# The bilinear products of a graph layer in 32-row pieces: four column groups of TensorE in place of two

## The chip, the cores and the metric

The kernel runs on one NeuronCore of one Trainium2 chip. The metric is the device time of one execution in microseconds (us), median of 3 runs. One profiled execution gives the trace from which all rows are read.

## The reference

The input is x, 128 graphs of 64 nodes with 384 features, and adj, 128 matrices of 64 x 64 edge weights. Four residual blocks follow one another, each `x = x + block(relu(layernorm(x)), adj)`. Block L0 is an attention with 12 heads and adj as bias, L2 a directed graph layer done twice, L3 an attention with adj as mask. The change touches block L1 alone, a graph layer done twice (l = 0, 1):

```
m_left = h @ W_left[l].T;  m_right = h @ W_right[l].T
u_left = h @ m_left.T / sqrt(384);  u_right = h @ m_right.T / sqrt(384)      # 64 x 64 for each graph
u = u_left * triu(adj, 0) + u_right * transpose(triu(adj, 1))
delta = exp(u) * adj;  attention = delta / (sum(delta, 2) + 1e-10)
h = relu(layer_norm(attention @ (h @ W_lin[l].T + b_lin[l])) * a + b)
```

So of u_left only the entries on and above the diagonal count, and of u_right only those below it: of the 128 numbers that the two forms give for a node, the masks keep 64.

## The kernel before, in words

One program for one core runs the four blocks as phases, one after the other. Each phase takes the 8192 rows (128 graphs of 64 nodes) in 16 groups of 512 rows: 4 tiles of 128 rows, two graphs to a tile. Products with weights (`split_matmul`, L52) are made of three fp32r matmuls each, with operands split in a high and a low part. Products of activations with one another run in plain fp32.

The second phase is `bilinear_phase` (block L1). Its unit of work is one layer of one group, 32 units in all, numbered `number(i, k)`; k = 0 to 3 are group 0 and 1 of a turn in the first layer, then both in the second. The opening unit stands by itself, then a loop runs units k = 1, 2, 3, 4 seven times, and the last three units close. Each engine has its own hand-written order, and semaphores tie them. A unit is, on TensorE (`unit` in `@block.tensor`):

- six products `product(i, k, j)`, 9 matmuls of 512 columns each: m_left and m_right, transposed, into the PSUM tiles `psW[0]`, `psW[1]`; ScalarE copies each into the SBUF tile `m` (`m_part`, L1252);
- behind the last three of them a set of four 128 x 128 transposes each (`passed`, L1495) of the next unit's rows into `psT`; ScalarE writes them out twice (`hT_part`, L1245 or L1248) and VectorE makes the low part `hT_lo` (L1349);
- `linear(0)`, 9 matmuls of 384 columns, read out by VectorE (`lin_copy`, L1363);
- `bilinear(i, k, t)` for the four tiles t (L1530): for each tile, each of the 3 chunks c of 128 features and each graph g of the tile one fp32 matmul, whose stationary operand is the 64 nodes of h (`hT_whole`) and whose moving operand is the left and the right m of the same 64 nodes, 128 columns. The result goes to partitions 64g to 64g + 63 of `psU`;
- `linear(1)`, `linear(2)`, `linear(3)`;
- `context` (L1554), delta times the linear rows, 8 fp32 matmuls.

VectorE multiplies `psU` by the masks (`mask_u`, L1357), adds the halves (L1359), ScalarE takes the exponential (L1256), VectorE multiplies by adj (`weigh_adj`, L1368), and only then may `context` run. VectorE's order in a unit is: the statistics of the unit before, `passed(0)`, `passed(1)`, `passed(2)` (each a subtraction for `hT_lo`), `lin_copy(0)`, `mask_u`, `lin_copy(1)`, `weigh_adj`, `lin_copy(2)`, `lin_copy(3)`. GpSimd makes the masks ahead of time (`make_masks`, L1176) and does the roots and the affine part of the second layer's output.

The lines that the change works on:

```
m = sb("m", [P, 2, KC, COLS])
for c in range(KC):
    for g in range(2):
        nodes = slice(t * P + g * NODES, t * P + (g + 1) * NODES)
        ins = nc.tensor.matmul(psU[NODES * g:NODES * (g + 1), t * P:(t + 1) * P].rearrange("p (s n) -> p s n", s=2),
                               hT_whole[k % 2][:, c, nodes], m[:, :, c, nodes], ...)
```

In the trace an fp32 matmul of the program is two MATMUL records and two LDWEIGHTS records: the 24 matmuls of a unit's bilinear form are 48 records of each. A transpose is one record.

Of the kernel before, what the change touches and what calls it, by code (L numbers as in the profile page):

```python
# [21 lines left out]
ACT = mybir.ActivationFunctionType  # L22
AX = mybir.AxisListType

P = 128
GRAPHS, NODES, D = 128, 64, 384
KC = D // P
ROWS = GRAPHS * NODES
TILES = 4
COLS = TILES * P  # L30
# [946 lines left out]
def bilinear_phase(nc, ctx, shared, x_in, adj, adjT, x_out, a, next_weights):  # L977
# [2 lines left out]
    n_w = 6  # L980
    eps, var_scale = 1e-3, float(D) / (D - 1)
    PAIR = TILES // 2

    def sb(n, shape, dt=F32):
        return ctx.enter_context(nc.sbuf_tensor(f"l1_{n}", shape, dt))
# [4 lines left out]
    def sem(n):  # L990
        return ctx.enter_context(nc.semaphore(f"l1_{n}"))
# [2 lines left out]
    xr = [sb(f"xr{g}", [P, TILES, D]) for g in range(2)]  # L994
    hT = [(sb(f"hT{b}_hi", [P, KC, COLS], F32R), sb(f"hT{b}_lo", [P, KC, COLS], F32R)) for b in range(2)]
    hT_whole = [sb(f"hT_whole{b}", [P, KC, COLS]) for b in range(2)]
    m = sb("m", [P, 2, KC, COLS])

    rows_of = [sb(f"adj{k}", [P, TILES, NODES]) for k in range(4)]
    cols_of = [sb(f"adjT{k}", [P, TILES, NODES]) for k in range(4)]  # L1000
# [41 lines left out]
    m_done = sem("m_done")  # L1042
    m_set = sem("m_set")
    masks_set = sem("masks_set")
    u_done = sem("u_done")
    u_read = sem("u_read")
    u_set = sem("u_set")
# [24 lines left out]
    def is_first(i, k):  # L1072
        return isinstance(i, int) and i == 0 and k == 0
# [74 lines left out]
    @block.gpsimd  # L1148
    def _(pool):
        nc.gpsimd.memset(half[:, 0:1], -0.5).then_inc(zeroed, 1)  # L1150
        nc.gpsimd.memset(half[:, 1:2], 0.5).then_inc(zeroed, 1)
        nc.gpsimd.memset(lin[:, :, D:D + 1], 1.0).then_inc(zeroed, 1)
        nc.gpsimd.memset(tri[:], 1.0).then_inc(zeroed, 1)
        pool.wait_ge(zeroed, 4)

        def roots(i, g):
            pool.wait_ge(var_set, 2 * i + g + 1)
            nc.gpsimd.tensor_tensor(rstd[:, g, :], var[:, g, :], half[:, 0:1].broadcast_to([P, TILES]), ALU.pow)\
              .then_inc(rstd_set, 1)

        roots(0, 0)
        pool.wait_ge(rstd_set, 1)
        for s, (sign, compare) in enumerate(((-1, ALU.is_ge), (1, ALU.is_gt))):
            for g in range(2):
                part = tri[NODES * g:NODES * (g + 1), s, :]
                nc.gpsimd.affine_select(out=part, in_=part, compare_op=compare, fill=0.0, base=0,
                                        pattern=[[sign, NODES]], channel_multiplier=-sign).then_inc(zeroed, 1)
                pool.wait_ge(zeroed, 4 + 2 * s + g + 1)
        roots(0, 1)

        def make_masks(i, k):

            per_turn = 64 if k < 2 else 128
            pool.wait_ge(adj_in[k], i * per_turn + per_turn)
            for side, source in enumerate((cols_of[k], rows_of[k])):
                nc.gpsimd.tensor_tensor(masks[k][:, :, side, :], source[:],  # L1176
                                        tri[:, side:side + 1, :].broadcast_to([P, TILES, NODES]), ALU.mult)\
                  .then_inc(masks_set, 1)

        def root(i, k, p):  # L1180
            pool.wait_ge(c_var_set, 2 * number(i, k) + p + 1)
            pair = slice(PAIR * p, PAIR * (p + 1))
            nc.gpsimd.tensor_tensor(c_root[:, pair], c_mv[:, pair, 1], half[:, 1:2].broadcast_to([P, PAIR]), ALU.pow)\  # L1183
              .then_inc(c_root_set, 1)

        def affine(i, k, x):
            pool.wait_ge(rows_set, number(i, k) * TILES + x + 1)
            nc.gpsimd.tensor_tensor(act_rows[:, x, :], act_rows[:, x, :], ln_a[:], ALU.mult).then_inc(affine_set, 1)
            pool.wait_ge(affine_set, 2 * ((2 * i + k - 2) * TILES + x) + 1)
            nc.gpsimd.tensor_tensor(act_rows[:, x, :], act_rows[:, x, :], ln_b[:], ALU.add).then_inc(affine_set, 1)  # L1190

        def ending(i, k):

            root(i, k, 0)
            root(i, k, 1)
            if k >= 2:
                for x in range(TILES):
                    affine(i, k, x)

        def unit(i, k, ahead):  # L1200
            ending(i, k - 1)
            if ahead and k in (1, 2):
                roots(i + 1, k - 1)
            if ahead:
                make_masks(i + 1, k - 1)

        pool.wait_ge(consts, 80)
        for k in range(4):
            make_masks(0, k)

        def turn(i, ahead):
            for k in (1, 2, 3, 4):
                if k < 4:
                    unit(i, k, ahead)
                elif ahead:
                    unit(i, k, ahead)
                else:
                    ending(i, 3)

        with pool.Fori(0, last) as i:  # L1220
            turn(i, True)
        turn(last, False)

    @block.scalar
    def _(act):
# [23 lines left out]

        def m_part(i, k, j):  # L1250
            act.wait_ge(m_done, number(i, k) * 2 * KC + j + 1)
            nc.scalar.activation(m[:, j // KC, j % KC, :], psW[j % 2][:], ACT.Copy).then_inc(m_set, 1)  # L1252

        def exponential(i, k):
            act.wait_ge(u_set, number(i, k) + 1)
# [61 lines left out]
    def _(dve):  # L1317
# [43 lines left out]
        def lin_copy(i, k, t):  # L1361
            dve.wait_ge(lin_done, number(i, k) * TILES + t + 1)
            nc.vector.tensor_tensor(lin[:, t, 0:D], psW[t % 2][:, 0:D], b_lin[:, k % 4 // 2, :], ALU.add)\  # L1363
              .then_inc(lin_set, 1)
# [28 lines left out]
        def result(i, k, x):  # L1393
            g = k - 2
            if x == 0:
                dve.wait_ge(xr_in[g], (i + 1) * 16)
            dve.wait_ge(affine_set, 2 * ((2 * i + g) * TILES + x + 1))
            nc.vector.scalar_tensor_tensor(xr[g][:, x, :], act_rows[:, x, :], 0.0, xr[g][:, x, :], ALU.max, ALU.add)\
              .then_inc(y_set, 1)
# [8 lines left out]
        def unit(i, k, ahead):  # L1408
            tail = not is_first(i, k)
            nexts = k < 3 or ahead  # L1410

            def passed(c):
                if nexts:
                    hT_part((number(i, k) + 1) * KC + c, (k + 1) % 2, c)

            if tail:
                ending(i, k - 1)
            if ahead and k in (1, 2):
                statistics((i + 1, k - 1))
                variances(k - 1)  # L1420
            passed(0)
            passed(1)
            if ahead and k in (1, 2):
                shifts((i + 1, k - 1))
            if tail and k >= 3:
                result(i, k - 1, 0)
                result(i, k - 1, 1)
            passed(2)
            lin_copy(i, k, 0)
            mask_u(i, k)  # L1430
            lin_copy(i, k, 1)
            weigh_adj(i, k)
            lin_copy(i, k, 2)
            lin_copy(i, k, 3)
            if tail and k >= 3:
                result(i, k - 1, 2)
                result(i, k - 1, 3)

        statistics((0, 0))
        variances(0)  # L1440
        weights((0,))
        shifts((0, 0))
        statistics((0, 1))
# [28 lines left out]
    def _(pe):  # L1472
# [48 lines left out]
        def bilinear(i, k, t):  # L1521
            n = number(i, k)
            if t == 0:
                wait_apart(m_set, (n + 1) * 2 * KC)
                if not is_first(i, k):
                    wait_apart(u_read, n)
            for c in range(KC):
                for g in range(2):
                    nodes = slice(t * P + g * NODES, t * P + (g + 1) * NODES)
                    ins = nc.tensor.matmul(psU[NODES * g:NODES * (g + 1), t * P:(t + 1) * P].rearrange("p (s n) -> p s n", s=2),  # L1530
                                           hT_whole[k % 2][:, c, nodes], m[:, :, c, nodes],
                                           start=(c == 0), stop=(c == KC - 1))
            if t == TILES - 1:
                ins.then_inc(u_done, 1)

# [23 lines left out]
        def unit(i, k, ahead):  # L1559
            nexts = k < 3 or ahead  # L1560
            if not is_first(i, k):
                pe.wait_ge(hT_set, (number(i, k) + 1) * KC)
            if is_first(i, k):
                pe.wait_ge(w_lo_set, LEFT + 1)
            for j in range(2 * KC):
                if is_first(i, k) and j == KC:
                    pe.wait_ge(w_lo_set, RIGHT + 1)
                product(i, k, j)
                if nexts and j >= KC:
                    passed(i, k, j - KC)  # L1570
            if is_first(i, k):
                pe.wait_ge(w_lo_set, LIN + 1)
            linear(i, k, 0)
            for t in range(TILES):
                bilinear(i, k, t)
            linear(i, k, 1)
            linear(i, k, 2)
            linear(i, k, 3)
            context(i, k, 0)
            context(i, k, 1)  # L1580
# [848 lines left out]
```

## Time and profile before

| | |
|---|---|
| median of 3 runs | 2840.08 us (2840.01 to 2840.34) |
| the profiled execution | 2840.32 us |
| its span in the trace | 2838.6 us |
| TensorE (PE) busy | 2708.2 us, 95% of the span |
| VectorE (DVE) busy | 1802.0 us, 63% |
| ScalarE (ACT) busy | 1256.7 us, 44% |
| GpSimd (POOL) busy | 1093.8 us, 39% |
| mean granted TensorE clock | 0.978 |
| HBM read, written | 131.61 MB, 50.33 MB |

The profiled execution took 0.24 us more than the median of the runs, and 1.7 us more than its span. Busy shares are averages over four phases. PE is matrix multiplication, PEld its weight loads, which run beside it. A row of a timeline has a start, the time from the first start to the last end of the instructions merged in it, and their count (x48); a single MATMUL record lasts longer than the time until the next may start, since records overlap.

### The profile page before, as it was taken

The page shows a single profiled execution, that of the slowest core. Times are in us where ns is not written, and L with a number is a line of the kernel's source. Part 1 is how long each engine was busy: PE and PEld are TensorE (multiplying, and loading weights), DVE is VectorE, ACT ScalarE, POOL GpSimd, SP SyncE. Part 2 cuts the span into 40 slices and gives each one's busy share as a digit, 9 for nine tenths or more (in the row PEclk, how much of TensorE's full clock was granted, in tenths as well). Part 3 has the DMA queues.
Part 4 walks back from the last instruction along what each step waited for, and adds up shares of the span by engine and source line. Part 5 has one row for each costly group of instructions (what it writes and reads, how often), then busy time and mean ns, then how long its engine had stood idle before and what let it go on. Part 6 is the DMA issues. An engine that isn't in the chain of part 4 may idle for free. (4 is left out here: it accounts for less than half of the span.)

```text
span 2838.6 us, 75948 instructions
## 1 busy us (share of the span) xinstructions
PE 2708.2 (95%) x29582; PEld 2345.1 (83%) x29582; DVE 1802.0 (63%) x4227; ACT 1256.7 (44%) x2212; POOL 1093.8 (39%) x1081
## 2 busy tenths in 40 slices
PE   6999999986999999999958999999999978999998
PEld 5888888875888888888847888888888867888887
DVE  5777777764445545544546787787777765666565
ACT  3444444434443444444433334343343325565564
POOL 2333333342323322332232444443444443545455
PEclk9999999998999999999988999999999988999999
DMA  4222222214112112211121111111111112222221
GB/s 139 71 70 66 65 62 62 67 51 150 35 56 78 41 45 76 78 33 55 48 80 43 51 50 50 49 60 39 55 55 48 49 52 72 79 91 80 84 89 59
DMA packets 186659, 183.15 MB, mean 65 GB/s; under 512 B 79568, under 2 KB 186064, under 8 KB 186576
## 3 DMA queue, kind: packets, MB, share of 16 engines
q1 hardware_dynamic: 186576, 181.99, 20.9%
q8 instruction: 59, 0.97, 0.1%
q14 instruction: 24, 0.20, 0.0%
HBM read 131.61 MB, written 50.33 MB: 64 GB/s over the span
## 5 line engine op out<-in xcount | busy, mean ns | idle before, releaser
L52 PE MATMUL l_psW<-w_hi,l_hT_hi 128*128 128x384 f32 x1920 | 681.7, 355 | 2.0 <-DVE l_vX L573 2.0
L52 PE MATMUL l_psW<-w_hi,l_hT_lo 128*128 128x384 f32 x1920 | 647.6, 337 | 0.0
L52 PE MATMUL l_psW<-w_lo,l_hT_hi 128*128 128x384 f32 x1920 | 645.2, 336 | 0.0
L52 PE MATMUL l_psW<-l_hT_hi,w_hi 128*128 128x512 f32 (+1 forms) x1242 | 495.7, 399 | 12.1 <-ACT l_m L1252 3.7
L52 PE MATMUL l_psW<-l_hT_hi,w_lo 128*128 128x512 f32 (+1 forms) x1242 | 469.8, 378 | 0.0
L52 PE MATMUL l_psW<-l_hT_lo,w_hi 128*128 128x512 f32 (+1 forms) x1242 | 469.1, 378 | 0.0
L52 PEld LDWEIGHTS l_psW<-w_hi,l_hT_hi 128*128 128x128 f32 x1920 | 362.0, 189 | 38.5 <-issue 24.6
L52 PEld LDWEIGHTS l_psW<-w_lo,l_hT_hi 128*128 128x128 f32 x1920 | 362.6, 189 | 0.7
L52 PEld LDWEIGHTS l_psW<-w_hi,l_hT_lo 128*128 128x128 f32 x1920 | 361.4, 188 | 0.0
L52 PEld LDWEIGHTS l_psW<-l_hT_hi,w_hi 128*128 128x128 f32 x1242 | 236.0, 190 | 69.6 <-issue 22.1
L52 PEld LDWEIGHTS l_psW<-l_hT_hi,w_lo 128*128 128x128 f32 x1242 | 235.5, 190 | 44.8
L52 PEld LDWEIGHTS l_psW<-l_hT_lo,w_hi 128*128 128x128 f32 x1242 | 236.8, 191 | 35.3
L284 POOL TENSOR_TENSOR l_s_d<-l_s_b,l_mx 128x768 f32<-128x768 f32 x128 | 188.9, 1476 | 195.4 <-DVE l_mx L561 182.4
L1252 ACT ACTIVATE l_m<-l_psW 128x512 f32<-128x512 f32 x192 | 114.7, 598 | 324.0 <-PE l_psW L52 324.0
L1349 DVE TENSOR_TENSOR l_hT_lo<-l_hT_whole,l_hT_hi 128x512 fp32r<-128x512 f32 x96 | 87.4, 910 | 251.6 <-ACT l_hT_whole L1245 128.0
L1183 POOL TENSOR_TENSOR l_c_root<-l_c_mv,l_half 128x2 f32<-128x2 f32 x64 | 44.7, 698 | 461.7 <-DVE l_c_mv L1380 461.7
L1824 POOL TENSOR_TENSOR l_right<-l_right,l_b_r 128x384 f32<-128x384 f32 x128 | 132.4, 1038 | 113.3 <-ACT l_right L1902 113.3
L1829 POOL TENSOR_TENSOR l_c_scale<-l_c_var,l_half 128x2 f32<-128x2 f32 x64 | 51.5, 804 | 319.2 <-DVE l_c_var L2052 319.2
L295 POOL TENSOR_TENSOR l_xr<-l_xr,l_y_rows 128x384 f32<-128x384 f32 x64 | 64.2, 1003 | 258.8 <-ACT l_y_rows L401 258.8
L387 ACT ACTIVATE l_eT<-l_psP 128x768 f32<-128x768 f32 x128 | 104.0, 813 | 129.8 <-PE l_psP L750 126.4
L761 PEld LDWEIGHTS l_psS<-l_vX,l_eT 64*64 64x64 f32 x6144 | 103.1, 136 | 41.0 <-issue 37.1
L573 DVE TENSOR_TENSOR l_vX<-l_psW,l_bv 64x192 f32<-64x192 f32 x256 | 90.8, 355 | 61.0 <-PE l_psW L52 58.1
(160 smaller groups left out, 5145.8 us busy)
## 6 DMA issues: line engine op xcount, KB each, us to landing
after_l<-l_xr SPq DMA_DIRECT2D x192, 192.0 KB, 1.9
l_xl<-after_l SPq DMA_DIRECT2D x47, 768.0 KB, 4.7
l_xr<-after_l SPq DMA_DIRECT2D x32, 768.0 KB, 4.5
l_xl<-in_x SPq DMA_DIRECT2D x16, 768.0 KB, 4.8
l_xr<-in_x SPq DMA_DIRECT2D x64, 192.0 KB, 2.4
l_xr<-after_l SPq DMA_DIRECT2D x64, 192.0 KB, 2.3
out_x<-l_xr SPq DMA_DIRECT2D x64, 192.0 KB, 1.9
l_adj<-in_adj SPq DMA_DIRECT2D x48, 128.0 KB, 2.4
```

The costliest lines, as they stand in the source:

```text
L52: last = nc.tensor.matmul(out, lhs[a](c), rhs[b](c), start=(m == 0), stop=(m == n - 1))
L284: nc.gpsimd.tensor_tensor(s_d[:], s_b[:, t], mx[:, t, :].rearrange("p (h n) -> p h n", n=1).broadcast_to([P, HEADS, NODES]), ALU.subtract) ...
L295: nc.gpsimd.tensor_tensor(xr[:, t, :], xr[:, t, :], y_rows[:, t % 2, :], ALU.add).then_inc(y_set, 1)
L387: nc.scalar.activation(eT[:, :, :].rearrange("p a n -> p (a n)"), P_all, ACT.Copy).then_inc(eT_set, 1)
L573: ins = nc.vector.tensor_tensor(vX[part, t, g, :, 0:HD], src[:, :, b, :], bias, ALU.add)
L761: ins = nc.tensor.matmul(psS[NODES * g:NODES * (g + 1), r, S_end + c * (HD + 1):S_end + (c + 1) * (HD + 1)], eT[keys_b, a, NODES * g:NODES ...
L1183: nc.gpsimd.tensor_tensor(c_root[:, pair], c_mv[:, pair, 1], half[:, 1:2].broadcast_to([P, PAIR]), ALU.pow)\
L1252: nc.scalar.activation(m[:, j // KC, j % KC, :], psW[j % 2][:], ACT.Copy).then_inc(m_set, 1)
L1349: nc.vector.tensor_tensor(hT[b][1][:, c, :], hT_whole[b][:, c, :], hT[b][0][:, c, :].bitcast(F32), ALU.subtract)\
L1824: nc.gpsimd.tensor_tensor(right[:, t, :], right[:, t, :], b_r[:, u.layer, :], ALU.add).then_inc(right_set, 1)
L1829: nc.gpsimd.tensor_tensor(c_scale[:, pair], c_var[:, pair], half[:].broadcast_to([P, PAIR]), ALU.pow)\
```

## The change

The bilinear form is cut in halves of the nodes. The stationary operand is 32 nodes instead of 64, so that each matmul writes 32 partitions of `psU`, and the four matmuls of a tile and chunk (two graphs, two halves) write partitions 0 to 31, 32 to 63, 64 to 95 and 96 to 127. The tile `m` is laid out anew, with the 64 right columns of a graph ahead of its 64 left ones. The first half of the nodes then needs columns 0 to 95 of these 128 (all of the right, the first half of the left), the second half columns 32 to 127. So each matmul has 96 moving columns in place of 128, and a unit has 48 matmuls in place of 24. The 32 columns for each row that are no longer written are zero times mask: `psU` is set to zero once, on VectorE, at the start of the phase, and TensorE waits for that before the first form. The masks swap their two sides in the same way.

The last set of transposes, `passed(KC - 1)`, moves from behind the last product to behind `linear(0)`, just ahead of the bilinear form. VectorE's `lin_copy(0)` moves ahead of its `passed(2)`.

```diff
+    HALF = NODES // 2
...
-    m = sb("m", [P, 2, KC, COLS])
+    m = sb("m", [P, KC, 2 * TILES, 2, NODES])
...
+    u_zeroed = sem("u_zeroed")
...
-                nc.gpsimd.tensor_tensor(masks[k][:, :, side, :], source[:],
+                nc.gpsimd.tensor_tensor(masks[k][:, :, 1 - side, :], source[:],
...
-            nc.scalar.activation(m[:, j // KC, j % KC, :], psW[j % 2][:], ACT.Copy).then_inc(m_set, 1)
+            nc.scalar.activation(m[:, j % KC, :, 1 - j // KC, :], psW[j % 2][:].rearrange("p (g n) -> p g n", n=NODES),
+                                 ACT.Copy).then_inc(m_set, 1)
...
+            lin_copy(i, k, 0)
             passed(2)
-            lin_copy(i, k, 0)
             mask_u(i, k)
...
+        nc.vector.memset(psU[:], 0.0).then_inc(u_zeroed, 1)
         weights((0,))
...
-                if not is_first(i, k):
+                if is_first(i, k):
+                    wait_apart(u_zeroed, 1)
+                else:
                     wait_apart(u_read, n)
             for c in range(KC):
                 for g in range(2):
-                    nodes = slice(t * P + g * NODES, t * P + (g + 1) * NODES)
-                    ins = nc.tensor.matmul(psU[NODES * g:NODES * (g + 1), t * P:(t + 1) * P].rearrange("p (s n) -> p s n", s=2),
-                                           hT_whole[k % 2][:, c, nodes], m[:, :, c, nodes],
-                                           start=(c == 0), stop=(c == KC - 1))
+                    both = m[:, c, 2 * t + g].rearrange("p s n -> p (s n)")
+                    for lower in range(2):
+                        first = g * NODES + lower * HALF
+                        cols = slice(lower * HALF, lower * HALF + NODES + HALF)
+                        ins = nc.tensor.matmul(psU[first:first + HALF, t * P + cols.start:t * P + cols.stop],
+                                               hT_whole[k % 2][:, c, t * P + first:t * P + first + HALF], both[:, cols],
+                                               start=(c == 0), stop=(c == KC - 1))
...
-                if nexts and j >= KC:
+                if nexts and KC <= j < 2 * KC - 1:
                     passed(i, k, j - KC)
...
             linear(i, k, 0)
+            if nexts:
+                passed(i, k, KC - 1)
             for t in range(TILES):
                 bilinear(i, k, t)
```

TensorE, a unit of the loop, from the end of the last product to the start of `linear(1)`. Before (a row is one matmul of the program, or xN alike; ISA is a wait that stands by itself):

```order
L52 MATMUL l_psW<-l_hT_hi,w_lo 128x512
L1493 ISA
L1495 MATMUL l_psT<-ident,l_act_rows 128x128 x4
L1539 ISA
L52 MATMUL l_psW<-w_hi,l_hT_hi 128x384
L52 MATMUL l_psW<-w_lo,l_hT_hi 128x384
...
L52 MATMUL l_psW<-w_hi,l_hT_lo 128x384
L1530 MATMUL l_psU<-l_m,l_hT_whole 64x128 x24
L52 MATMUL l_psW<-w_hi,l_hT_hi 128x384
```

With the change:

```order
L52 MATMUL l_psW<-l_hT_hi,w_lo 128x512
L1548 ISA
L52 MATMUL l_psW<-w_hi,l_hT_hi 128x384
L52 MATMUL l_psW<-w_lo,l_hT_hi 128x384
...
L52 MATMUL l_psW<-w_hi,l_hT_lo 128x384
L1497 ISA
L1499 MATMUL l_psT<-ident,l_act_rows 128x128 x4
L1539 MATMUL l_psU<-l_m,l_hT_whole 32x96 x48
L52 MATMUL l_psW<-w_hi,l_hT_hi 128x384
```

The 24 matmuls of 64 x 128 (output rows x columns) have become 48 of 32 x 96, and the four transposes have moved past `linear(0)` to stand directly ahead of them.

VectorE, the same stretch in the opening unit. Before:

```order
L1349 TENSOR_TENSOR l_hT_lo<-l_hT_whole,l_hT_hi 128x512 x3
L1363 TENSOR_TENSOR l_lin<-l_psW,l_b_lin 128x384
L1357 TENSOR_TENSOR l_u_parts<-l_psU,l_masks 128x512
L1359 TENSOR_TENSOR l_u_sum<-l_u_parts 128x256
L1363 TENSOR_TENSOR l_lin<-l_psW,l_b_lin 128x384
L1368 TENSOR_TENSOR l_delta<-l_e_u,l_adjT 128x256
```

With the change:

```order
L1352 TENSOR_TENSOR l_hT_lo<-l_hT_whole,l_hT_hi 128x512 x2
L1366 TENSOR_TENSOR l_lin<-l_psW,l_b_lin 128x384
L1352 TENSOR_TENSOR l_hT_lo<-l_hT_whole,l_hT_hi 128x512
L1360 TENSOR_TENSOR l_u_parts<-l_psU,l_masks 128x512
L1362 TENSOR_TENSOR l_u_sum<-l_u_parts 128x256
L1366 TENSOR_TENSOR l_lin<-l_psW,l_b_lin 128x384
```

The third subtraction for `hT_lo` now stands between the copy of `linear(0)` and the masking of `psU`.

## Rows read from the trace of the kernel before

**Rows 1.** The page, busy time of the engines over the span

```profile
PE 2708.2 (95%) x29582; PEld 2345.1 (83%) x29582; DVE 1802.0 (63%) x4227; ACT 1256.7 (44%) x2212; POOL 1093.8 (39%) x1081
```

**Rows 2.** Stretches, 684.00:1459.90 is the second phase from its first form

```profile
core 0: us, PE busy (x) PEld busy (x) DVE busy (x) ACT busy (x) POOL busy (x), PEclk, DMA share, GB/s
684.00:1459.90 775.90, 774.49 (x5225) 641.83 (x5225) 386.34 (x1025) 333.33 (x578) 234.70 (x252) 1.00 0.18 53
```

**Rows 3.** Waits of the PE in that stretch: the only one

```profile
PE l_psC L1554 <- issue: 0.2, 1, 0.2
```

**Rows 4.** Timeline of the PE, one unit, from the last product on

```profile
start us, us, engine line op out<-in xcount [idle before <-releaser]
1003.64 0.40 PE L52 MATMUL l_psW<-l_hT_hi,w_lo 128*128 128x512 f32 x1
1003.88 0.60 PE L1495 MATMUL l_psT<-ident,l_act_rows 128*128 128x128 f32 x4
1004.23 0.42 PE L52 MATMUL l_psW<-w_hi,l_hT_hi 128*128 128x384 f32 x1
1004.49 0.34 PE L52 MATMUL l_psW<-w_lo,l_hT_hi 128*128 128x384 f32 x1
...
1005.71 0.34 PE L52 MATMUL l_psW<-w_hi,l_hT_lo 128*128 128x384 f32 x1
1005.98 2.84 PE L1530 MATMUL l_psU<-l_m,l_hT_whole 128*64 128x128 f32 x48
1008.75 0.44 PE L52 MATMUL l_psW<-w_hi,l_hT_hi 128*128 128x384 f32 x1
1009.03 0.33 PE L52 MATMUL l_psW<-w_lo,l_hT_hi 128*128 128x384 f32 x1
...
1013.65 1.89 PE L1554 MATMUL l_psC<-l_lin,l_delta 64*64 64x385 f32 x16
```

**Rows 5.** The tile psU: durations in ns, minimum/median/maximum

```profile
L1530 PE MATMUL l_psU<-l_m,l_hT_whole x1536: 272/273/324, 683.9 to 1453.4; 128*64 128x128 f32 x192
L2199 PE MATMUL l_psU<-l_hT_whole x1536: 221/222/367, 1494.7 to 2302.0; 128*64 128x64 f32 x192
```

**Rows 6.** The line of the context, the same columns

```profile
L1554 PE MATMUL l_psC<-l_lin,l_delta x512: 482/494/536, 691.6 to 1459.9; 64*64 64x385 f32 x171
```

**Rows 7.** Timeline of the PE in the third phase, its u in 64 columns

```profile
1530.08 1.62 PE L2199 MATMUL l_psU<-l_hT_whole 128*64 128x64 f32 x48
```

**Rows 8.** Timeline of the PE in the first phase, scores and weighing

```profile
102.57 0.90 PE L761 MATMUL l_psS<-l_vX,l_eT 64*64 64x33 f32 x48
...
119.15 1.28 PE L743 MATMUL l_psS<-l_kT,l_qT 32*64 32x64 f32 x96
```

**Rows 9.** The line of the scores, durations in ns

```profile
L743 PE MATMUL l_psS<-l_kT,l_qT x6144: 210/218/365, 36.6 to 2820.7; 32*64 32x64 f32 x199
```

**Rows 10.** Timeline of the weight loads beside the form of that unit

```profile
1005.98 2.60 PEld L1530 LDWEIGHTS l_psU<-l_m,l_hT_whole 128*64 128x64 f32 x48 [0.25 <-issue]
```

**Rows 11.** Timeline of ACT in that unit

```profile
1004.07 0.60 ACT L1252 ACTIVATE l_m<-l_psW 128x512 f32<-128x512 f32 x1 [0.59 <-PE l_psW L52]
1004.57 0.77 ACT L1245 ACTIVATE l_hT_hi<-l_psT,l_ln_bT,l_ln_aT 128x512 fp32r<-128x512 f32 x1
1005.23 0.78 ACT L1245 ACTIVATE l_hT_whole<-l_psT,l_ln_bT,l_ln_aT 128x512 f32<-128x512 f32 x1
```

**Rows 12.** Timeline of DVE in that unit

```profile
1006.04 0.69 DVE L1349 TENSOR_TENSOR l_hT_lo<-l_hT_whole,l_hT_hi 128x512 fp32r<-128x512 f32 x1 [1.76 <-ACT l_hT_whole L1245]
...
1008.94 0.69 DVE L1357 TENSOR_TENSOR l_u_parts<-l_psU,l_masks 128x512 f32<-128x512 f32 x1 [1.74 <-PE l_psU L1530]
...
1011.11 0.41 DVE L1368 TENSOR_TENSOR l_delta<-l_e_u,l_adjT 128x256 f32<-128x256 f32 x1
```

**Rows 13.** Timeline of DVE at the start of the phase

```profile
648.41 1.35 DVE L1324 TENSOR_TENSOR w_lo<-w_raw,w_hi 128x1152 fp32r<-128x1152 f32 x1
650.67 0.16 DVE L1344 SCALAR_TENSOR_TENSOR l_nbias<-l_mv,l_rstd 128x4 f32<-128x4 f32 x1 [0.91 <-POOL l_rstd L1158]
```

## Prediction

> **What bounds the kernel now.** I read the page first, then the stretch of the phase that the change touches, then the waits in it, then one unit in order of time. The page has PE busy for 95% of the span, and no other engine above 63% [rows 1]. Averages over four phases prove little, so the stretch decides: from the first bilinear form of the second phase to its end PE is busy 774.49 of 775.90 us, at a granted clock of 1.00, that is 2.4 GHz, while DVE works 386, ACT 333 and POOL 235 us [rows 2]. In all of it PE waited once, 0.2 us [rows 3]. So the second phase is PE's own work laid end to end, and a microsecond taken from PE there comes off the span, as long as nothing else becomes late. The reader is to see in the unit's timeline that the bilinear form starts at 1005.98, and the next matmul stands at 1008.75: 2.8 us in each of 32 units, some 90 us of the phase [rows 4].
>
> **What a record of the form costs.** An fp32 record of 128 columns lasts 272 ns at the least, one of 64 columns 221, one of 385 columns 482 [rows 5, 6]. That is 0.80 to 0.82 ns for each further column, two cycles at 2.4 GHz, so 128 columns hold their part of the array for about 107 ns; the rest is latency that overlaps. 48 records one after another would take 48 x 107 ns = 5.1 us. The form takes 2.84 us from first start to last end, less 0.27 for the last record: 2.57 us from first start to last start [rows 4, 5]. So two records, those of graph 0 and graph 1 on partitions 0 to 63 and 64 to 127, run at a time: 24 rounds at some 107 to 109 ns. The third phase's form, the same 48 records of 128 rows and 64 output rows with 64 columns, takes 1.62 - 0.22 = 1.40 us, 24 rounds at 58 ns [rows 5, 7].
>
> **The change, part by part.**
>
> 1. *The form.* 96 records, each on a quarter of the array's output side, with 96 moving columns. If four run at a time as two do now, that is again 24 rounds, now of 96 columns. The trace has such rounds for 64 columns (1.40 us) and for 128 (2.57 us), and 96 is halfway: 1.98 us from first to last start, and the last record lasts 247 ns in place of 273. Saved are 2.57 - 1.98 = 0.59, plus 0.03, together 0.61 us in each unit; 32 units give **19.6 us**. Both ends of this term come from the same rows: four starts in a round in place of two cost a few ns more or less. If a round is 3 ns off, the 24 x 32 rounds give 2.3 us either way.
>
> 2. *Do four run at a time?* No row of 128 rows of stationary data shows more than two. What is nearest: the scores run eight pieces of 32 x 64, 96 records in 1.28 - 0.22 = 1.06 us, 11 ns to a record, and the weighing four pieces of 64 x 64, 48 records in 0.90 - 0.22 = 0.68 us, 14 ns to a record [rows 5, 8, 9]. So the array does run four and eight at a time, and starts come far closer than the 1.98 us / 96 = 21 ns that the new form wants. But in both of these at most two records read the same partitions at once, in the new form four do. I take four at a time, because pieces side by side are what every such row shows; what it is worth if it fails is below.
>
> 3. *The weight loads.* 96 loads of 32 columns in place of 48 of 64, the same columns in all. They lie beside the matmuls now: 48 loads fill 2.60 us inside the form's 2.84 [rows 4, 10]. In the 64-column form two loads of 64 columns fit in every 58 ns. A round of the new form has four loads of 32 columns, as many columns, and 83 ns. If loads go by columns, they are covered: zero. If they went by the piece, they would not be (a rival, below).
>
> 4. *The transposes, moved.* In their old place they cost their own work: from their start at 1003.88 to the second matmul behind them at 1004.49 is 0.61 us, four at 109 ns and one matmul at 0.17 [rows 4]. Into the form some 0.10 us is lost (0.27 from the last start of linear(0), less 0.17), and behind it 0.20 us (1008.55 last start, plus 0.11, to 1009.03 less 0.17). The change of the array's pieces happens as often as before. Behind transposes the way into the form could cost nothing, or twice as much: 31 units x 0.10 us, 3.1 us either way. I take zero, since all that changes is which full-array work stands ahead.
>
> 5. *What becomes late by that move.* The third pair of ACT writes started at 1004.57, 0.7 us behind the start of its transposes, and ended at 1006.01 [rows 4, 11]. The transposes now start nine matmuls later, 1.57 us, so ACT ends near 1007.6, and DVE's subtraction, 0.69 us, near 1008.3 [rows 12]. It now stands ahead of the masking. The form ends 0.61 us earlier, and masking, which started at 1008.94, could start at 1008.33 [rows 12]. Hence a delay of 0.0 to 0.1 us for DVE. Who waits for it: the exponential, then delta at 1011.11 to 1011.52, then the context on PE at 1013.65, 2.1 us later [rows 4, 12]. That cover holds also when both ends move 0.6 us forward. The first unit's `hT_lo` is wanted only by the next unit's products, 6 us later. Zero. Were the cover gone, each 0.1 us would cost 3 us.
>
> 6. *Copies, masks, zeroing.* ACT writes m in eight pieces of 64 columns; at 0.60 us against a product's 2.1 us and with ACT at 43% of the stretch, some 10% more would be hidden [rows 2, 11]. The masks only swap sides. The zeroing of `psU` is one DVE instruction on 512 columns, not longer than the 0.69 us that masking the same tile takes [rows 12]. It stands ahead of the split of the first weights, behind which DVE waits 0.91 us for POOL's root [rows 13]. Zero, at most a tenth.
>
> Sum: 2840.3 us of the profiled execution less 19.6 gives 2820.7; the median of the runs stands 0.2 lower, so **2820.5 us**. In this case alone the range is 2815 to 2826 (2.3 for the rounds, 3.1 for the transposes).
>
> **Rivals.**
>
> - *Four cannot run at a time on the same 128 partitions, two can.* Then 96 records of 96 columns are 48 rounds at 83 ns, 4.0 us, against 2.57: 1.4 us more in each unit, 46 us in all: **2886 us**. For it: two is the most that any row has on one partition. Against it: nothing in the trace shows a limit at two; it is only never tried. It decides the sign: with s records at a time the form takes 96 x 83 ns / s, which is 2.57 us at s = 3.1. So below three at a time the change loses. Chance 0.07.
> - *A record has a price of its own.* The densest starts of records with 128 rows are 1.40 us / 48 = 29 ns [rows 7]. If that is the price of a load or a start whatever its columns, 96 of them take 2.79 us, 0.2 us more than now, **2847 us**. Against it stand the 11 and 14 ns of the first phase [rows 8], with fewer rows. Chance 0.06. The Trainium skill, page "TensorE: Matmul & The Clock Gate", section "Wait — 56ns, not 53.3ns?", states such a floor: start to start never below about 25 ns. By that the form would take 96 x 25 ns = 2.4 us, and the kernel some 2834 us; by the scores' 11 ns the trace does not agree.
> - *Four run, but each round is stretched* (reads of four streams, or loads between them) to about 97 ns, halfway back to the present one: half the gain, **2830 us**. Chance 0.07.
> - *The gain is taken back by a new wait*, or the records keep running in pairs at the old total: PE's 0.6 us turns up as idle time ahead of the context or of linear(3). The 2.1 us of cover speaks against it. **2840 us**. Chance 0.06.
>
> **How the numbers follow.** The forecast's case has 0.74. A measurement of this kernel can tell about 0.2%, 5.7 us, from no change. Faster: 0.74 + 0.07 = 0.81. Within 0.2%: 0.06, and a little of the rival at 2847, which lies just beyond: 0.08. Slower: the rest of the two rivals above, 0.11. The range runs from 2814, a little below the case's own low end, to 2840, which takes in the half gain and the gain taken back; left out are the two slower rivals and some error of the main case.
>
> **What the changed profile would show.** Right: the form as one PE row x96 of 2.2 us, records of 96 columns at about 247 ns, units 0.6 us shorter, PE waiting nowhere, the context's start the same distance behind linear(3). Wrong: a form row of 2.8 us (price by the record) or 4 us and more (two at a time); idle time of PE with DVE's delta or ACT as its releaser; masking later than 0.2 us behind the form's end; a granted clock below 1.00 in the stretch.

## The result and the profile after

The changed kernel takes 2889.32 us (median of 4 runs, 2886.84 to 2891.01) against 2840.21 us before (four runs too): ratio 1.0173, 95% interval 1.016 to 1.0186. It is 49 us slower; 2820.5 had been forecast, within 2814 to 2840.

The form itself did what the forecast said. The tile `psU` in the profile after, columns as in [rows 5]:

```profile
L1539 PEld LDWEIGHTS l_psU<-l_m,l_hT_whole x3072: 106/110/110, 683.2 to 1499.7; 128*32 128x32 f32 x192
L1539 PE MATMUL l_psU<-l_m,l_hT_whole x3072: 246/246/271, 683.2 to 1499.8; 128*32 128x96 f32 x192
```

A record lasts 246 ns (247 foreseen). The timeline of the PE after, at the last form of the first pass of the loop and at the context behind it:

```profile
779.15 0.60 PE L1499 MATMUL l_psT<-ident,l_xl 128*128 128x128 f32 x4
779.68 2.19 PE L1539 MATMUL l_psU<-l_m,l_hT_whole 128*32 128x96 f32 x96
...
786.41 0.34 PE L52 MATMUL l_psW<-w_hi,l_hT_lo 128*128 128x384 f32 x1
786.68 1.65 PE L1563 MATMUL l_psC<-l_lin,l_delta 64*64 64x385 f32 x16
791.88 0.49 PE L52 MATMUL l_psW<-l_hT_hi,w_hi 128*128 128x512 f32 x1 [3.56 <-issue]
792.21 0.40 PE L52 MATMUL l_psW<-l_hT_lo,w_hi 128*128 128x512 f32 x1
798.10 0.79 PE L52 MATMUL l_psW<-l_hT_hi,w_lo 128*128 128x512 f32 x1 [5.49 <-issue]
798.69 0.63 PE L52 MATMUL l_psW<-l_hT_hi,w_hi 128*128 128x512 f32 x1
799.12 0.63 PE L52 MATMUL l_psW<-l_hT_lo,w_hi 128*128 128x512 f32 x1
```

96 records in 2.19 us, where 48 took 2.84 [rows 4]. But then PE stands still, for 3.6 us and, two matmuls later, for 5.5 us, and runs at half speed after it: eleven matmuls of 512 columns follow, nearly all at 0.43 us where 0.23 is usual. What it waits for is called "issue": nothing that the profile shows. Before, the same place looked like this:

```profile
790.74 1.64 PE L1554 MATMUL l_psC<-l_lin,l_delta 64*64 64x385 f32 x16
792.31 0.50 PE L52 MATMUL l_psW<-l_hT_hi,w_hi 128*128 128x512 f32 x1
792.65 0.40 PE L52 MATMUL l_psW<-l_hT_lo,w_hi 128*128 128x512 f32 x1
```

It is the jump back of TensorE's loop over the turns. The trace has the branch that closes the loop (seven times, the seventh not taken; ns minimum/median/maximum), before and after:

```profile
L1595 PEldq COMPARE_BRANCH  x7: 76/208/221, 791.6 to 1386.2; - x7
```

```profile
L1606 PEldq COMPARE_BRANCH  x7: 76/3730/5465, 787.6 to 1434.5; - x7
```

The branch itself takes 3.6 to 5.5 us at each of the six jumps, where it took 0.2. The waits of the PE in the second phase after, where [rows 3] had one of 0.2 us:

```profile
PE l_psW L52 <- issue: 50.5, 12, 5.6
```

Twelve waits, two at each of the six jumps. Stretches after: the last unit ahead of the jump from the end of its form on, the jump with what follows, and the next unit.

```profile
core 0: us, PE busy (x) PEld busy (x) DVE busy (x) ACT busy (x) POOL busy (x), PEclk, DMA share, GB/s
781.70:787.90 6.20, 6.20 (x52) 5.08 (x43) 3.68 (x8) 0.42 (x1) 0.00 (x0) 1.00 0.11 25
787.90:815.40 27.50, 18.45 (x83) 14.49 (x75) 7.89 (x31) 8.53 (x14) 3.78 (x5) 0.81 0.37 120
815.50:839.80 24.30, 24.17 (x215) 19.91 (x214) 11.62 (x38) 10.39 (x17) 3.80 (x5) 1.00 0.05 12
```

The granted clock is 0.81 in the middle one. From the start of one form to the start of the next, units away from a jump take 24.03 us, one in four 24.33 (24.69 and 24.98 before), and those across one 34.4 to 36.5 (24.7 before). The sum agrees: 32 x 0.65 = 21 us are gained and 68 us lost at the six jumps together, 47 us more; the spans differ by 46.4.

Part 3 of the profile's page shows it once more. The queue that brings instructions (packets, MB, share), before and after:

```profile
q8 instruction: 59, 0.97, 0.1%
```

```profile
q8 instruction: 118, 1.93, 0.3%
```

It is 16.4 kB a packet in both. Between two jumps of the changed kernel nine such packets arrive (ten behind the second jump and behind the third), and none between the first two of the kernel before. Counted in the trace from one branch of the loop to the next, TensorE's instructions (matmuls, weight loads, waits, registers) are 1418 in a pass before and 1802 now: 4 units with 24 more matmuls, of 2 records and 2 loads each.

### The profile page after: what moved, and what is told of

It reads as the page before. It is cut to its first block and busy times, and to the rows that moved or that the text cites. A ratio compares the mean times of both kernels' runs of the same rounds, so it can differ in the third digit from the quotient of the medians.

```text
span 2885.0 us, 79022 instructions
## 1 busy us (share of the span) xinstructions
PE 2702.1 (94%) x31118; PEld 2335.5 (81%) x31118; DVE 1796.9 (62%) x4228; ACT 1260.1 (44%) x2212; POOL 1094.4 (38%) x1081
## 5 line engine op out<-in xcount | busy, mean ns | idle before, releaser
L52 PE MATMUL l_psW<-l_hT_hi,w_lo 128*128 128x512 f32 (+1 forms) x1242 | 476.0, 383 | 27.3 <-issue 27.3
L1352 DVE TENSOR_TENSOR l_hT_lo<-l_hT_whole,l_hT_hi 128x512 fp32r<-128x512 f32 x96 | 80.0, 833 | 312.8 <-ACT l_hT_whole L1247 187.6
L1366 DVE TENSOR_TENSOR l_lin<-l_psW,l_b_lin 128x384 f32<-128x384 f32 x128 | 71.2, 556 | 96.8 <-PE l_psW L52 96.8
```

The lines of the kernel that those rows point to most:

```text
L52: last = nc.tensor.matmul(out, lhs[a](c), rhs[b](c), start=(m == 0), stop=(m == n - 1))
L1352: nc.vector.tensor_tensor(hT[b][1][:, c, :], hT_whole[b][:, c, :], hT[b][0][:, c, :].bitcast(F32), ALU.subtract)\
```

## The experiments

Three theories: **F**, a jump back in a loop that is too long for what TensorE keeps of its program must fetch it again; **C**, the stalls belong to the 32-row form; **M**, they belong to the moved transposes. Each group of runs had the kernel before run on the same chip, 2839.5, 2839.8 and 2839.1 us in the three groups.

**e1_before_twice**

```diff
-        with pe.Fori(0, last) as i:
-            turn(i, True)
+        with pe.Fori(0, last // 2) as i:
+            turn(i + i, True)
+            turn(i + i + 1, True)
+        if last % 2:
+            turn(last - 1, True)
```

> The kernel before, its matmuls and their order untouched; only TensorE's loop in the second phase has two turns in its body (2836 instructions of TensorE by the trace's count of 1418 for one) and runs 3 times, the seventh turn stands behind it. Theory F (the jump back of a loop whose body is too long for what TensorE keeps costs a fetch, some 11 us in the changed kernel): two jumps back, about 2 x 9 to 11 us, so 2858 to 2863 us, with two places in which PE waits some 4 and 6 us for nothing that the profile shows. Theory C (the stalls belong to the 32-row form, its column groups or the data it reads): no stall, 2840 us. Theory M (they belong to the moved transposes): 2840 us.

2849.19 us, ratio 1.0035 (1.0024 to 1.0047). The waits of the PE in the phase:

```profile
PE l_psW L52 <- issue: 6.7, 2, 3.4
```

The matmuls of the kernel before, with no 32-row form and no move, stall once the loop is longer: F, not C or M. But they stall only once at each of the two jumps, and in the profiled execution, the slowest of the seven, the unit across it takes 30.8 to 30.9 us, 6.1 more and not 11. The median is 9 us below the low end of what was expected. That miss led to theory B below.

**e2_after_unrolled**: the changed kernel, `for i in range(last): turn(i, True)` in place of the loop.

> The changed kernel, with TensorE's loop of the second phase written out seven times, no jump back; everything else as changed. Theory F: the stalls of 9 to 12 us at six places go, the form's gain of 0.66 us a unit stays: 2889.3 - 6 x 11.2 = 2822 us at most, nearer 2819 (2840.2 - 32 x 0.66). Theory C or M: the stalls stay, 2885 to 2890 us. If straight code cannot be fetched as fast as it runs, there are stalls all along the phase, and more than 2840 us.

2825.53 us, 0.9949 (0.9932 to 0.9965). No stall is left at these places; the straight code was fetched as fast as it ran. It missed 2819 to 2822 since most units took 24.3 us, not 24.03 (e8).

**e3_same_count**

```diff
-            for c in range(KC):
-                for g in range(2):
...
+            for s in range(2):
+                for c in range(KC):
+                    for g in range(2):
...
+                        first = t * P + s * NODES
+                        ins = nc.tensor.matmul(psU[NODES * g:NODES * (g + 1), first:first + NODES],
+                                               hT_whole[k % 2][:, c, nodes], m[:, s, c, nodes],
```

> The kernel before, the form cut in two by columns: 48 matmuls of 64 rows x 64 columns for a unit (first the left, then the right), transposes and DVE order as before, m as before. As many instructions as the changed kernel (1802 in the loop's body), but only two column groups. The form takes 48 rounds of 58 ns, 2.8 us, in place of 2.57: +0.2 us in each of 32 units, +7. Theory F: the six jumps back cost 9 to 11 us each on top: 2900 to 2913 us. Theory C: no stalls, 2847 us. Theory M: no stalls, 2847 us.

2911.54 us, 1.0255 (1.0238 to 1.0272). The form is in two column groups as before, and only the count of instructions is that of the change. The twelve waits are back:

```profile
PE l_psW L52 <- issue: 51.6, 12, 5.5
```

**e4_moves_alone**: the diff of the change without its form, its m and its masks.

> The kernel before with the moves of the change alone: the last transposes behind linear(0), lin_copy(0) ahead of passed(2); the form as before, 64 rows x 128 columns. Theory F and theory C: 2840 us, 3 us at most either way, no stall. Theory M: stalls at the six jumps, some 2900 us.

2840.12 us, 1.0002 (0.9993 to 1.0012), with no stall. M has fallen, and the moves are worth nothing either way.

**How long is too long?** In the next three the 32-row form stands in one, two or three of the loop's four units:

```diff
+                    if not is_first(i, k) and not (isinstance(i, int)) and k in (1, 2, 3):
+                        first = g * NODES
+                        ins = nc.tensor.matmul(psU[first:first + NODES, t * P:(t + 1) * P],
+                                               hT_whole[k % 2][:, c, t * P + first:t * P + first + NODES], both,
+                                               start=(c == 0), stop=(c == KC - 1))
+                        continue
```

(`k in (1, 2)` in the second, `(1,)` in the third.)

> The changed kernel, but in the loop's body only k = 4 has the 32-row form, k = 1, 2, 3 have 64 rows x 128 columns (in the new layout of m). TensorE's body is about 1514 instructions (1418 + 96). Theory F with a limit on the whole body somewhere between 1418 (no stall) and 1802 (two stalls at each jump): here most likely none, time 2840 - 11 units (7 in the loop, 4 outside) x 0.66 = 2833 us. If the limit is just above 1418: six stalls of 6 to 11 us, 2870 us and more.

> As e5, with the 32-row form at k = 3 and 4, body about 1610 instructions. Theory F: without stalls 2840 - 18 x 0.66 = 2828 us; with them 2865 to 2895 us. That one of the two happens, and not a slow rise with the count, is what theory F says.

> As e5, with the 32-row form at k = 2, 3 and 4, body about 1706 instructions. Theory F: without stalls 2840 - 25 x 0.66 = 2823.5 us; with them 2860 to 2890 us. I expect the stalls here: with the turn before it still partly held, 1706 instructions are nearer to the 1802 that did not fit.

e5 takes 2833.19 us (0.9967 to 0.9988 of before) with 1514 instructions in a pass, e6 2896.35 (1.0181 to 1.0222) with 1610, e7 2895.31 (1.0178 to 1.0218) with 1706. It is a step, not a slope: 96 instructions more cost 63 us. e6 and e7 lie 1 and 5 us above what was expected with stalls.

**e8_unrolled_lin_last**: e2, and in `context`

```diff
             wait_apart(d_set, n + 1)
-            wait_apart(lin_set, n * TILES + PAIR * (p + 1))
             if not is_first(i, k):
                 wait_apart(rows_set, (n - 1) * TILES + PAIR * (p + 1))
+            wait_apart(lin_set, n * TILES + PAIR * (p + 1))
```

> The changed kernel with TensorE's loop written out (as e2) and, in context(), the wait for the linear rows put last, behind the wait for the act_rows. In e2 each unit took 24.28 us where the loop's k = 3 and 4 took 24.03: the wait for the linear rows, which comes last in time, has a further wait instruction behind it there. If that order is the cause: 0.25 us less in some 30 units, 2818 us. If it isn't: 2825.5 us as e2.

2817.23 us, 0.9925 (0.9908 to 0.9941): the fastest kernel here, 22.6 us under the one before. Units take 24.04 to 24.08 us, and the 16 records of a context 1.69 us where e2 needs 1.90. A wait that ends last should stand last: each wait behind it is still to be worked off when it ends. The phase in e8, to be held against [rows 2]:

```profile
core 0: us, PE busy (x) PEld busy (x) DVE busy (x) ACT busy (x) POOL busy (x), PEclk, DMA share, GB/s
684.00:1440.00 756.00, 753.56 (x6765) 624.59 (x6763) 384.88 (x1036) 337.66 (x580) 235.74 (x253) 1.00 0.19 56
```

**Where the loop lies.** In the changed kernel, e6 and e7 the second stall came two weight loads and two matmuls behind the first, whatever the length. In e3, whose loop starts one instruction earlier in the program, one load more fitted in between: the same place in the program. e1, whose loop starts 97 instructions earlier than that of the change (its opening unit has the old form), had no second stall. Theory **B**: the program comes in blocks of one packet, 16.4 kB. How many instructions that is, the runs show: the kernel before with its loop written out (e11, below) has some 8200 more of them in TensorE's program and 32 more packets (91 against 59), 257 to a packet. The Trainium skill, page "Runtime: NRT & Kernel Launch", section "Instruction fetch mechanics", says that an instruction memory is refilled in blocks of 16 KiB, 256 instructions, that TensorE's holds 2048, and that a taken branch out of the current window of two of them waits for a fetch. Packet size and stalls here agree with the blocks and the branch. The window of two blocks, 512 instructions, is not borne out for TensorE: loops of 1418 and 1514 jump back without a stall. The next two runs leave the loop alone and change the unit ahead of it: e9 is the changed kernel, e10 is e6, both with the opening unit in the form of 64 rows x 128 columns. The condition for that form, in e9 and in e10:

```diff
+                    if is_first(i, k):
...
+                    if is_first(i, k) or not (isinstance(i, int)) and k in (1, 2):
```

> The changed kernel, but the opening unit, which stands ahead of the loop, keeps the form of 64 rows x 128 columns: 96 instructions of TensorE fewer ahead of the loop, the loop's body the same 1802. Theory B (instructions come in blocks of 256, 16.4 kB a packet on the instruction queue; a jump back waits for the block with the loop's start, and again for the next block if the start lies at the end of its block, as the second stall 4 instructions behind the first shows): the start now lies 100 instructions ahead of the block's end, these run while the next block comes, and the second stall of some 6 us and part of the slow clock go: unit 6.1 us longer at each of six jumps as in e1, not 11: 2840 - 31 x 0.66 + 6 x 6.1 = 2856 us. Theory L (only the length of the body counts): 2889 us, both stalls.

> e6 (32-row form at k = 3 and 4 of the loop, body 1610, which stalled: 2896 us) with the opening unit in the form of 64 rows x 128 columns. Theory B: with its start 4 instructions ahead of a block's end the body of e6 touches 1 + 7 blocks, that of e5 (1514, no stall) 1 + 6; with the start 100 ahead of the end, 1610 touches 1 + 6 blocks again. If seven blocks stay and eight don't, e10 has no stall: 2840 - 17 x 0.66 = 2829 us. Theory L (the limit is a length between 1514 and 1610 wherever the body lies): it stalls, 2860 to 2896 us.

e9: 2851.78 us, 1.0044 (1.0028 to 1.0061), with one wait a jump; the units across a jump take 27.2 to 30.2 us.

```profile
PE l_psW L52 <- issue: 19.9, 6, 3.7
```

It lies 4 us under the 2856 expected, since a jump costs 5.2 us on average and not 6.1. Two of these units, across the fourth and the fifth jump, show what the clock adds:

```profile
core 0: us, PE busy (x) PEld busy (x) DVE busy (x) ACT busy (x) POOL busy (x), PEclk, DMA share, GB/s
1088.10:1118.30 30.20, 26.51 (x216) 21.67 (x214) 13.41 (x41) 10.04 (x17) 5.03 (x7) 0.89 0.38 115
1190.70:1218.00 27.30, 24.20 (x219) 19.94 (x217) 13.47 (x41) 10.03 (x17) 5.03 (x7) 1.00 0.41 127
```

At a granted clock of 1.00 the jump costs 3.2 us, its stall of 3.1 and no more; at 0.89 it costs 6.1, with a stall of 3.7.

e10: 2827.71 us, 0.9958 (0.9941 to 0.9974), with no wait at the jumps; a unit across one takes 24.08 us. It is the same loop as in e6, which took 2896.35. The instruction queue in e10, and in one pass of e6 (789.3 to 898.1):

```profile
q8 instruction: 61, 1.00, 0.2%
```

```profile
q8 instruction: 9, 0.15, 0.5%
```

In e10 none arrives between one jump and the next, in e6 nine in every pass: there the loop is fetched anew each time.

So one unit *outside* the loop, made 0.65 us slower, takes 69 us off the kernel. A length alone (theory L) cannot explain it. Nor can the place of the loop's start alone: e5 starts where e6 does and does not stall, e9 starts where e10 does and stalls. The number of blocks that the loop touches can. If a block ends where the second stall falls, the loop's first block holds 6 of its instructions in the change, e5, e6 and e7, 7 in e3, and 102 or 103 in the others; so e6 touches 1 block and, with its other 1604 instructions, 7 more, and e10 1 block and, with 1508, 6 more. Seven are kept (before, e4, e5, e10); eight (e6, e7, e9), nine (the change and e3, by four and three instructions) or twelve (e1) are not.

**e11_before_unrolled_lin_last**: both edits of e8 on the kernel before.

> The control for e8: the kernel before with TensorE's loop written out and the wait for the linear rows put last, the form in 64 rows x 128 columns, no moves. If the gain of e8 is the form's: this kernel gains only 0.25 to 0.3 us in the eleven units or so that had that wait in the middle, 2837 us, and e8 (2817.2) stays 20 us ahead. If it was the missing jumps: 2820 us.

2838.33 us, 0.9995 (0.9985 to 1.0005). Against e8 it is 21.1 us slower: that is the form's gain, 32 x 0.66, since the moves are worth nothing (e4). By themselves the two edits gave the kernel before nothing clear of noise: nearly all its units take 24.73 us, where one in four took 24.98 and two in four 24.69.

## Why the prediction was wrong

- *What bounds the kernel.* "a microsecond taken from PE there comes off the span, as long as nothing else becomes late". This is the step that failed. The sum asked of DVE, ACT and GpSimd whether they would be late, and not of what brings PE its instructions. Part 3 of the prediction set down "96 loads of 32 columns in place of 48 of 64", priced them in the array, and stopped. Nobody counted that the loop grows from 1418 to 1802 instructions. That term, put at nothing, measured 68 us: 10.3 to 12.4 us at each of six jumps. The rows could not give the price, since every jump before was free; but the instruction queue's 59 packets stood on the page, and the price of a jump that is not free should have been a rival.
- *Four at a time, and the size of the term.* Right. 1.94 us from first to last start where 1.98 was foreseen, 0.65 us a unit where 0.61 was. The rounds come every 83 ns.
- *The loads.* Right: covered. The rival of 29 ns a record has fallen, with 1.94 us / 96 = 20 ns. So has the floor of 25 ns that the prediction quoted from the Trainium skill, page "TensorE: Matmul & The Clock Gate": the trace does not agree, for records in four column groups.
- *Two at a time, 2886 us.* The measured 2889 us lies next to this rival by accident. It foretold a form of 4 us, and the form takes 2.19.
- *The moves.* Right: zero (e4). In the timeline of DVE after, in a unit whose form starts at 731.62, the masking follows the third subtraction at once, and delta is ready at 736.5, 2.1 us ahead of the context at 738.62:

```profile
733.20 0.69 DVE L1352 TENSOR_TENSOR l_hT_lo<-l_hT_whole,l_hT_hi 128x512 fp32r<-128x512 f32 x1 [1.36 <-ACT l_hT_whole L1247]
733.94 0.69 DVE L1360 TENSOR_TENSOR l_u_parts<-l_psU,l_masks 128x512 f32<-128x512 f32 x1
...
736.08 0.41 DVE L1371 TENSOR_TENSOR l_delta<-l_e_u,l_adjT 128x256 f32<-128x256 f32 x1
```

- *A gain taken back by a new wait.* The kind was named, with the wrong place (the context or linear(3)) and the price of the gain alone. The wait here costs 68 us, three times what was gained.
- *What would make it wrong.* The list had "a granted clock below 1.00 in the stretch", and so it is, but as a consequence: PE stood idle at the jump, and then ran at the lower of its two levels.

What stays open: how many instructions TensorE really holds, and why seven blocks and not eight. The runs show the step between seven and eight for these positions alone. A block fetched ahead of need beyond the loop's end would make eight of seven, but no run tested it; nor does the count of packets decide it, for nine arrive in a pass of e6, with eight blocks, and in most passes of the changed kernel, with nine. What sets the length of a stall was not tested either: data transfers share the time with the fetch (DMA share 0.79 from 787.9 to 791.9 in the changed kernel), and at two of its six jumps, the second and the third, the first stall was the longer one.

## What to carry to other kernels

Count the instructions of a loop's body on each engine before and after an edit, and find out whether the jump back is free: the timeline at the place where the loop closes shows it, as idle time put down to "issue". Where splitting work into more and smaller instructions pays in the array, the same edit can push the loop over the step; writing the loop out keeps the gain (e2, e8). Shifting the loop's start by the code ahead of it kept it only where the loop came down to seven blocks by it (e10), and not for the whole change (e9, 1.0044). And put the wait that ends last at the end of a row of waits.

## What was not expected of the hardware

A jump back in TensorE's loop is free, or costs 3.2 to 6.2 us with one stall (3.1 to 3.7 us in e1 and e9) or 10.3 to 12.4 us with two (7.7 to 9.3 us together), and which one depends on how long the loop is and on where in the program it starts. Not all of it is idle time: on average 3.3 us of 5.2 in e9, 8.4 us of 11.3 in the changed kernel. Most of the rest lies in the clock, whose grant over the 27.5 us around one jump was 0.81: there the eleven matmuls behind the second stall took 4.9 us in place of 2.5, which is 2.3 of the 2.7 us that were not idle time. TensorE runs four fp32 matmuls of 32 output rows on the same 128 partitions at a time, with rounds of 96 columns every 83 ns. Straight code of some 14000 instructions, at 18 a us, ran without a stall.
